# A graph layer on one core: gathering the input itself and normalising the gathered rows on the chip, instead of storing a normalised table first

## The chip, the cores and the metric

The kernel runs on one core of a Trainium2 chip (trn2). The metric is the device time of one execution in microseconds. The kernel before takes 2262.23 us, the median of three runs (2261.8 to 2264.33).

## What is computed

There are 12,500 nodes with rows of 256 numbers (x) and 212,500 edges, sorted by dst, each with a row of 64 numbers. Everything is float32. Cut to what matters:

```python
h = relu(layernorm(x, eps=1e-5))
messages = concat([h[src], edges]) @ W_message          # 320 -> 256
agg = segment_sum(messages, dst)
v = relu(agg) + h
u = layernorm(v) * aggr_scale + aggr_bias
u1 = u + relu(u @ W0 + b0)
u2 = u1 + relu(u1 @ W1 + b1)
w = h + (u2 + u2 @ W2 + b2)
out = x + layernorm(w) * out_scale + out_bias
```

Since the message layer is linear, the kernel first sums the rows of each node (320 numbers: h[src] and the edge row) and multiplies by W_message once for a block of 128 nodes.

## The kernel before

**Names.** A *block* is 128 nodes; there are 98 (NB). A *tile* is 128 edges in the order of dst; there are 1664 (T). Eight tiles (G) are a *group*; there are 208 (NG). A block has some 17 tiles, so its last edge falls into every second group, sometimes the third: that group *closes* the block. The work that follows a closing is a *visit*.

**First stage.** In 14 rounds (NX) of seven rows a partition, POOL loads x (L267), DVE takes mean and variance (`x_moments`: `bn_stats` L572, `bn_aggr` L581) and computes 1/std and the shift with one Newton step in six small operations (`x_scale`, L550 to L564), ACT takes the root (L431) and writes relu((x - mean) / std) in place (L437), and SP stores the rows to a table in HBM, h_table (L240). Between these rounds DVE builds the tables of numbers (`steer`, `whole`) from dst that tell each group in which accumulator each tile goes, whether the group closes a block and which.

**The stream.** When all of h_table is stored (the waits ahead of L274), POOL gathers, for each tile, 128 rows of h_table by src with an indirect DMA (L281) into `ring`, which has room for eight groups (RG); SP loads the edge rows of a group beside them (L248). Both wait for `group_free`, which PE counts up when it has used a group. DVE compares dst with the lane numbers and gets a 128x128 one-hot matrix for each tile (L670); PE multiplies it with the tile (L361) and so adds each edge's row to its node's in PSUM. PE waits for the gathers in pairs of tiles.

**The visits.** Each engine handles a visit in a place of its program that is the same as the group's: in a closing group PE does seven tiles, the visit, and the eighth tile (L372 to L378):

```python
for j in range(G - 1):
    tile(j)
...
with nc.tensor.If(closes > 0):
    pe_visit(pe, visit, ..., close)
tile(G - 1).then_inc(group_free, 1)
```

A visit is a step of a software pipeline over the blocks: it copies the sums of block n, and does each later layer for an earlier block, up to the output of block n - LAG (LAG = 5). PE's part (L301 to L332) transposes z (L305), closes the accumulator (L369), multiplies by W_message (L313), adds the last layer (L319), does two layers (L295) and transposes the sums (L330). ACT's part (`act_visit`) takes the root of the variances (L390), loads h of two blocks and x of one again from HBM (L392 to L395), copies and applies relu (L399 to L417) and stores the output (L406). DVE's part (`dve_visit`) adds, takes both norms with one Newton step, and writes z (L518) and the output (L520). After the last group come a full visit for the last block and LAG short ones.

**What sets the order.** Each engine runs its own program in order, and semaphores join them. DVE makes the one-hots of a group and then, if the group closes a block, does the visit. ACT has nothing but visits. POOL has nothing but gathers.

Of the kernel before, what the change touches and what calls it, by code (L numbers as in the profile page):

```python
# [6 lines left out]
F32 = mybir.dt.float32  # L7
BF16 = mybir.dt.bfloat16
I32 = mybir.dt.int32
# [12 lines left out]
PT = 2  # L22
XS = 4
LAG = 5
# [4 lines left out]
def sizes(n_nodes, n_edges):  # L29
    nb = -(-n_nodes // P)  # L30
    per_load = max(k for k in range(1, 8) if nb % k == 0)
    return nb, per_load, -(-n_edges // (P * GT)) * GT

def build(nc, x, src, dst, edges, w_message, w_mlp, feature_params, row_params, out, NB, XB, T):
# [3 lines left out]
    NX = NB // XB  # L39
    PAIRS = G // PT  # L40

    AT, VSEL, CLOSES, VISIT, TILE, W = G, G + 1, G + 2, G + 3, G + 4, G + 5
    PARAMS = 16 * 5

    h_table = nc.dram_tensor("h_table", (NB * P, D), F32, kind="Internal").ap()
    dump = nc.dram_tensor("dump", (P, D), F32, kind="Internal").ap()
    x_blocks = x.rearrange("(b p) d -> p b d", p=P)
    h_blocks = h_table.rearrange("(b p) d -> p b d", p=P)

    x_rows = x.rearrange("(p b) d -> p b d", p=P)  # L50
    h_rows = h_table.rearrange("(p b) d -> p b d", p=P)
# [3 lines left out]
    with ctx:  # L55
# [11 lines left out]
        close_hot = sb("close_hot", [P, P])  # L67
# [4 lines left out]
        xs = sb("xs", [P, XS, XB, D])  # L72

        flat = ring[:, :, :].rearrange("p j f -> p (j f)")
        dst_i = flat[:, 0:T].bitcast(I32)
        last_i = flat[:, T:2 * T].bitcast(I32)
        last_shifted = flat[:, 2 * T:3 * T].bitcast(I32)
        below = flat[:, 3 * T:4 * T]
        rel = flat[:, 4 * T:5 * T]
        blk_i = sb("blk_i", [1, T + 1], I32)  # L80
# [11 lines left out]
        parity_i = sb("parity_i", [1, NB], I32)  # L92
        parity = sb("parity", [1, NB])
# [4 lines left out]
        visit_sel = sb("visit_sel", [1, NB], I32)  # L98
# [12 lines left out]
        x_stats = sb("x_stats", [P, XB, 6])  # L111
        x_mv = sb("x_mv", [P, 2, XB, 2])
        x_var = sb("x_var", [P, XB])
        x_std = sb("x_std", [P, 2, XB])
        x_y = sb("x_y", [P, XB])
        x_t = sb("x_t", [P, XB])
        x_u = sb("x_u", [P, XB])
        x_rstd = sb("x_rstd", [P, 2, XB])
        x_shift = sb("x_shift", [P, 2, XB])
# [10 lines left out]
        h_in = sb("h_in", [P, D])  # L130
        h_late = sb("h_late", [P, D])
        x_late = sb("x_late", [P, D])
# [6 lines left out]
        w0 = sb("w0", [P, D])  # L139
        w = sb("w", [P, D])  # L140
        scaled = sb("scaled", [P, D])
        o = sb("o", [P, D])
        stats = sb("stats", [P, 2, 6])
        mv = sb("mv", [P, 2, 2])
# [88 lines left out]
        def _(sp):  # L233
# [19 lines left out]
            for s in range(XS):  # L253
                sp.wait_ge(h_stored[s], 16 * len(range(s, NX, XS)))
# [473 lines left out]
```

## Time and profile before

| | |
|---|---|
| median of 3 runs | 2262.23 us |
| the profiled execution | 2263.02 us, of which its span is 2261.2 us |
| mean clock granted to TensorE | 0.937 |
| PE busy, of the span | 74% |
| POOL | 71% |
| DVE | 42% |
| ACT | 16% |
| software DMA queue (the gathers), of 16 engines | 34.7% |

The profile is one execution, recorded on the chip. Times are microseconds from the start of the span unless marked ns. PE is TensorE's matmul, PEld its weight load, DVE is VectorE, ACT ScalarE, POOL GpSimd, SP SyncE; a q behind a name is that engine's queue of instructions that start DMAs.
### The profile page before, as it was taken

What the parts mean: (1) busy time and instruction counts of PE and PEld (TensorE: products, weight loads), DVE (VectorE), ACT (ScalarE), POOL (GpSimd) and SP (SyncE); (2) the same over time, 40 slices, a digit from 0 to 9 for tenths busy, and PEclk for the clock granted to TensorE, in tenths of its full rate; (3) what the DMA queues carried; (4) which work ended last, traced back from release to release, by engine and by line L of the source; (5) the groups of instructions that cost most, each with busy time, mean ns of one, the idle gap of its engine ahead of it and who ended that gap; (6) DMA issues with size and microseconds to landing.
All of it is one profiled execution on the core that took longest, in us unless ns stands there. A gap on an engine that the chain in (4) does not pass through costs nothing.

```text
span 2261.2 us, 35804 instructions
## 1 busy us (share of the span) xinstructions
PE 1672.8 (74%) x6729; PEld 1128.5 (50%) x6730; DVE 957.0 (42%) x3949; ACT 364.2 (16%) x1114; POOL 1594.7 (71%) x1687
## 2 busy tenths in 40 slices
PE   0058778878878777788778778778787887777876
PEld 0035545545555545555555555555554555555544
DVE  8444334434434434443433433443443434434434
ACT  2601111111111111111111111111111111111112
POOL 0067777777777777777777777777777777777770
PEclk9999999999999999999999999998998999999997
DMA  6775555555555555555555555555555555555542
GB/s 234 276 189 158 156 155 155 150 159 155 155 158 154 156 159 150 161 157 149 159 155 155 156 150 161 157 160 149 159 157 151 161 149 158 161 147 161 154 123 61
DMA packets 361302, 357.81 MB, mean 158 GB/s; under 512 B 250208, under 2 KB 303776, under 8 KB 361120
## 3 DMA queue, kind: packets, MB, share of 16 engines
q0 software_dynamic: 81888, 231.06, 34.7%
q1 hardware_dynamic: 218768, 69.94, 12.4%
q10 hardware_dynamic: 60464, 55.28, 7.3%
q14 instruction: 177, 1.45, 0.2%
q8 instruction: 5, 0.08, 0.0%
HBM read 329.65 MB, written 26.48 MB: 157 GB/s over the span
## 4 chain that ended last, share of the span: by engine, by line
POOL 62%; issue 21%; PE 8%; DMA 3%; DVE 1%; POOLq 0%; ACT 0%; DVEq 0%; ACTq 0%
POOL ring L281 62%; PE acc_banks L361 4%; DMA ring<-h_table,src_all 2%; PE agg_bank L313 1%; PE agg_bank L319 1%; PE y_bank L295 1%; PE z_bank L295 1%; PE acc_banks L369 0%; POOLq L277 0%; PE z_bank L305 0%; ACT xs L437 0%; DMA h_table<-xs 0%; PE st_bank L330 0%; POOLq L279 0%; ACT r_bank L411 0%
## 5 line engine op out<-in xcount | busy, mean ns | idle before, releaser
L281 POOL DMA_INDIRECT ring<-h_table,src_all x1664 | 1586.0, 953 | 527.2 <-issue 519.6
L361 PE MATMUL acc_banks<-ring,onehot 128*128 128x320 f32 x3328 | 1112.2, 483 | 518.8 <-issue 310.0
L361 PEld LDWEIGHTS acc_banks<-ring,onehot 128*128 128x128 f32 x3328 | 659.9, 209 | 933.5 <-issue 773.7
L670 DVE TENSOR_SCALAR onehot<-iota,dst_rel 128x128 f32<-128x128 f32 x1664 | 360.6, 303 | 249.2 <-issue 200.7
L480 DVE TENSOR_TENSOR w<-agg_bank,h_late 128x256 f32<-128x256 f32 x103 | 43.7, 424 | 953.8 <-PE agg_bank L319 953.8
L399 ACT ACTIVATE uT<-z_bank,fp 128x128 f32<-128x128 f32 x200 | 80.6, 453 | 1482.0 <-PE z_bank L305 1482.0
L313 PE MATMUL agg_bank<-wm,ST 128*128 128x256 f32 (+1 forms) x594 | 166.4, 401 | 0.0
L313 PEld LDWEIGHTS agg_bank<-wm,ST 128*128 128x128 f32 (+1 forms) x594 | 106.5, 192 | 54.9 <-issue 34.6
L319 PE MATMUL agg_bank<-wl,u 128*128 128x256 f32 x408 | 118.5, 414 | 6.3 <-DVE z L518 6.3
L295 PEld LDWEIGHTS y_bank<-u,wl 128*128 128x128 f32 x808 | 108.8, 196 | 5.6
L295 PE MATMUL y_bank<-u,wl 128*128 128x128 f32 x808 | 109.0, 279 | 0.0
L411 ACT ACTIVATE r_bank<-y_bank,fp 128x128 f32<-128x128 f32 x202 | 60.4, 338 | 298.2 <-PE y_bank L295 298.2
L295 PE MATMUL z_bank<-uT,wl 128*128 128x128 f32 x800 | 106.6, 277 | 0.0
L295 PEld LDWEIGHTS z_bank<-uT,wl 128*128 128x128 f32 x800 | 98.4, 194 | 0.0
L319 PEld LDWEIGHTS agg_bank<-wl,u 128*128 128x128 f32 x408 | 70.8, 193 | 45.8 <-issue 33.1
L369 PE MATMUL acc_banks<-ring,close_hot 128*128 x194 | 74.2, 465 | 0.0
L267 POOL DMA_DIRECT2D xs<-x x14 | 7.6, 549 | 88.9 <-DMA h_table<-xs 88.9
L411 ACT ACTIVATE r_bank<-z_bank,fp 128x128 f32<-128x128 f32 x200 | 59.8, 337 | 30.4 <-PE z_bank L295 30.4
L499 DVE TENSOR_TENSOR u<-u,r_bank 128x256 f32<-128x256 f32 x102 | 42.9, 421 | 20.8 <-ACT r_bank L411 19.9
L572 DVE BATCH_NORM_STATS2 x_stats<-xs 128x6 f32<-128x256 f32 x98 | 37.9, 411 | 30.9 <-DMA xs<-x 30.6
L437 ACT ACTIVATE xs<-xs,x_shift,x_rstd 128x256 f32<-128x256 f32 x98 | 49.4, 585 | 0.0
L520 DVE SCALAR_TENSOR_TENSOR o<-scaled,rstd,xb 128x256 f32<-128x256 f32 x103 | 49.3, 479 | 0.0
(109 smaller groups left out, 919.1 us busy)
## 6 DMA issues: line engine op xcount, KB each, us to landing
ring<-edges SPq DMA_DIRECT2D x208, 256.0 KB, 3.7
ring<-h_table,src_all POOLq DMA_INDIRECT x1664, 2.8
h_late<-h_table ACTq DMA_DIRECT2D x103, 128.0 KB
x_late<-x ACTq DMA_DIRECT2D x103, 128.0 KB
h_in<-h_table ACTq DMA_DIRECT2D x100, 128.0 KB
xs<-x POOLq DMA_DIRECT2D x14, 896.0 KB, 6.5
h_table<-xs SPq DMA_DIRECT2D x14, 896.0 KB, 4.2
out<-o ACTq DMA_DIRECT2D x98, 128.0 KB
```

The costliest lines, as they stand in the source:

```text
L281: nc.gpsimd.indirect_dma_start(out=ring[:, k * G + j, 0:D], out_offset=None, in_=h_table, in_offset=bass.IndirectOffsetOnAxis(ap=src_all[: ...
L295: mm = nc.tensor.matmul(y[layer][:, c * P:(c + 1) * P], wl[:, layer, k, c * P:(c + 1) * P], u[:, k * P:(k + 1) * P], start=(k == 0), stop= ...
L313: mm = nc.tensor.matmul(agg, ST[0:m, c, :], wm[0:m, c, :], start=(c == 0), stop=(c == 2))
L319: mm = nc.tensor.matmul(back, u2[:, k * P:(k + 1) * P], wl[:, 2, k, :], start=(k == 0), stop=(k == 1))
L361: return nc.tensor.matmul(acc_of(at), onehot[:, (k % OG) * G + j, :], ring[:, k * G + j, :], start=False, stop=True, skip_group_check=True)
L369: nc.tensor.matmul(acc_of(sel), close_hot[:, :], rhs, start=False, stop=True, skip_group_check=True).then_inc(block_closed, 1)
L399: op = nc.scalar.activation(uT[:, c * P:(c + 1) * P], zT[:, c * P:(c + 1) * P], ACT.Identity, scale=fp[:, 2, c:c + 1], bias=fp[:, 3, c:c + 1])
L411: op = nc.scalar.activation(r[layer][:, c * P:(c + 1) * P], y[layer][:, c * P:(c + 1) * P], ACT.Relu, bias=fp[:, layer, c:c + 1])
L437: op = nc.scalar.activation(at, at, ACT.Relu, scale=x_rstd[:, n % 2, k:k + 1], bias=x_shift[:, n % 2, k:k + 1])
L480: step(nc.vector.tensor_tensor(w0[:, :], back, h_late[:, :], ALU.add))
L520: nc.vector.scalar_tensor_tensor(o[:, :], scaled[:, :], rstd[:, 1:2], xb[:, :], ALU.mult, ALU.add).then_inc(out_ready, 1)
L670: op = nc.vector.tensor_scalar(onehot[:, (k % OG) * G + j, :], iota[:, :], dst_rel[:, bass.ds(g * G + j, 1)], None, ALU.is_equal)
```

## The change

- There is no first stage and no h_table. POOL gathers rows of x itself, and waits only for src, which SP now loads first.
- Each gathered tile is normalised in `ring`. DVE takes `bn_stats` of its eight tiles (L732) and `bn_aggr` (L739); ACT takes the root (L492) and normalises with relu (`apply`, L463 to L469); the six small operations of `x_scale` are five (`x_norms`: eps is added within the second) and stand between the statistics of the *next* group (`next(norms, None)`). ACT applies them at the head of its next group. PE waits for each half of a normalised group (`applied`), where it waited for pairs of gathers.
- ACT and DVE now walk through all groups. PE handles a visit in the closing group, ACT its middle part (`act_node`) one group later and its norms (`act_norms`) two later, DVE all of its part two groups later (BEHIND = 2).
- In a closing group's visit DVE puts the one-hots of its current group between the steps of the norms (`group_hots`, `next(others, None)`).
- A visit's 1/std is computed on DVE alone, from a first guess of integer arithmetic on the bits (MAGIC) and three Newton steps on three columns; the third is the norm of the block's own rows. ACT writes z, and the h of the block's own rows (`hr`) from x (`xr`), both kept in eight slots (HS) for four visits; only x of one block is loaded in a visit.
- PE adds h and b2 to the last layer by two more matmuls (L319, L320), where DVE did it. LAG is 4. The matmul that closes a block uses a one-hot from four buffers.
- The setup clears `xr`, `hr` and two more tables, and builds those.

The core of the diff:

```diff
-            for n in range(NX):
-                s = n % XS
-                if n >= XS:
-                    pool.wait_ge(h_stored[s], 16 * (n // XS))
-                pool.dma_start(xs[:, s, :, :], x_rows[:, n * XB:(n + 1) * XB, :]).then_inc(x_in[s], 16)
...
+            def gather(g):
+                k = g % RG
+                for j in range(G):
+                    nc.gpsimd.indirect_dma_start(
+                        out=ring[:, k * G + j, 0:D], out_offset=None, in_=x,
+                        in_offset=bass.IndirectOffsetOnAxis(ap=src_all[:, g, j:j + 1], axis=0),
+                    ).then_inc(gathered[2 * k + j // HALF], 16)
+            pool.wait_ge(src_in, 16)
+            for g in range(NG):
+                pool.wait_ge(group_free, g + 1)
+                gather(g)
...
+            def apply(k, count):
+                act.wait_ge(x_norm_ready, count + 2)
+                for j in range(G):
+                    at = ring[:, k * G + j, 0:D]
+                    op = nc.scalar.activation(at, at, ACT.Relu, scale=x_rstd[:, k % 2, j:j + 1], bias=x_shift[:, k % 2, j:j + 1])
+                    if j % HALF == HALF - 1:
+                        op.then_inc(applied, 1)
...
+                        looked = look_back(g)
+                        if not (first and k == 0):
+                            apply((k - 1) % RG, p * NG + g)
+                        act.wait_ge(x_moments_ready, p * NG + g + 2)
+                        nc.scalar.activation(x_std[:, k % 2, :], x_mv[:, k % 2, :, 1], ACT.Sqrt,
+                                             bias=x_eps[:, 0:1]).then_inc(x_std_ready, 1)
+                        visits(*looked)
...
+                        for j in range(G):
+                            if j % HALF == 0:
+                                wait_for(gathered[2 * k + j // HALF], (p * ROUNDS + i + 1) * (16 * HALF))
+                            op = nc.vector.bn_stats(x_stats[:, j, :], ring[:, k * G + j, 0:D])
+                            if j == G - 1:
+                                op.then_inc(x_stats_ready, 1)
+                            next(norms, None)
+                        wait_for(x_norm_ready, count + 1)
+                        wait_for(x_stats_ready, count + 1)
+                        for j in range(G):
+                            op = nc.vector.bn_aggr(x_mv[:, k % 2, j, :], x_stats[:, j, :])
+                        op.then_inc(x_moments_ready, 1)
+                        wait_for(group_free, count + 1 + RG - OG)
+                        with nc.vector.If(closes > 0):
+                            dve_visit(dve, visit, visit * STEPS, slots, group_hots(k, g, opened, tile))
+                            nc.vector.nop()
+                        with nc.vector.Else():
+                            for _ in group_hots(k, g, opened, tile):
+                                pass
+                            nc.vector.nop()
...
+            nc.tensor.matmul(back, ident[:, :], of_slot(hr, late), start=True, stop=False)
+            nc.tensor.matmul(back, ones[0:1, :], b2_row[0:1, :], start=False, stop=False)
+            for k in range(2):
+                mm = nc.tensor.matmul(back, u2[:, k * P:(k + 1) * P], wl[:, 2, k, :], start=False, stop=(k == 1))
```

The new DVE part of a visit, in the order of its code: v (L528), statistics of `back` (L529), then a wait for the last relu (`r_ready`), u2 (L532), statistics of the own rows (L535) and of v (L538), u1 (L541), three `bn_aggr` (L544), xb (L546), the variances (L548), scaled (L549), the first guess (L552), nine Newton operations (L557 to L563), shift (L566), o (L568).

**DVE, from the last Newton step of a visit to the next group.** `rt`, `ru`, `ry`/`rstd` are the small vectors of the norms, `z` goes to the next layer, `o` is the output, `onehot` the one-hots of the group. Before:

```order
L513 SCALAR_TENSOR_TENSOR ru<-rt,ry 128x2 [waits dve_step,tables]
L471 REGISTER_ALU
L515 SCALAR_TENSOR_TENSOR rstd<-ru,ry 128x2 [waits dve_step,tables]
L518 TENSOR_SCALAR z<-v,mv,rstd 128x256 [waits rstd_ready]
L520 SCALAR_TENSOR_TENSOR o<-scaled,rstd,xb 128x256 [waits out_stored]
L680 UNCONDITIONAL_BRANCH
L224 ISA
L224 TENSOR_LOAD steer
L225 ISA
L670 ISA [waits group_free]
L670 TENSOR_SCALAR onehot<-iota,dst_rel 128x128
```

With the change:

```order
L703 TENSOR_SCALAR onehot<-iota,dst_rel 128x128
L519 REGISTER_ALU
L560 SCALAR_TENSOR_TENSOR ru<-rt,ry 128x3 [waits dve_step,tables]
L703 TENSOR_SCALAR onehot<-iota,dst_rel 128x128
L519 REGISTER_ALU
L563 SCALAR_TENSOR_TENSOR ry<-ru,ry 128x3 [waits dve_step,tables]
L519 REGISTER_ALU
L566 SCALAR_TENSOR_TENSOR shift<-mv,ry 128x3 [waits dve_step,tables]
L568 SCALAR_TENSOR_TENSOR o<-scaled,ry,xb 128x256 [waits out_stored,tables]
```

The next group, past the branch, begins so; `x_stats` are the statistics of its gathered tiles and `x_y` is the first of the small vectors for the group before it:

```order
L207 TENSOR_LOAD dve_steer
L208 ISA
L732 BN_STATS x_stats<-ring 128x6 [waits tables,gathered4,x_moments_ready]
L683 RECIPROCAL x_y<-x_std 128x8 [waits x_std_ready,tables]
L732 BN_STATS x_stats<-ring 128x6
```

The one-hots of the group have moved in among the Newton steps, z has gone to ACT, and behind the output stand the next group's statistics with the norms of the group between them.

**PE, inside a visit.** `agg_bank` holds the message layer's result and, in its other half, `back`. Before:

```order
L369 MATMUL acc_banks<-ring,close_hot 128x320
L313 MATMUL agg_bank<-wm,ST 128x256 [waits ST_ready]
L313 MATMUL agg_bank<-wm,ST 128x256 x2
L319 MATMUL agg_bank<-wl,u 128x256 x2
L295 MATMUL y_bank<-u,wl 128x128 x4
L295 MATMUL z_bank<-uT,wl 128x128 [waits u_in]
```

With the change:

```order
L369 MATMUL acc_banks<-ring,close_hot 128x320
L316 MATMUL agg_bank<-wm,ST 128x256 [waits ST_ready]
L316 MATMUL agg_bank<-wm,ST 128x256 x2
L319 ISA
L319 MATMUL agg_bank<-hr,ident 128x256
L320 MATMUL agg_bank<-rows,ones 128x256
L322 MATMUL agg_bank<-wl,u 128x256 x2
L297 MATMUL y_bank<-u,wl 128x128 x4
L297 MATMUL z_bank<-uT,wl 128x128 [waits u_in]
```

Two matmuls now stand ahead of those of the last layer, and so ahead of both layers whose relu DVE waits for.

## Rows read from the trace of the kernel before

**Rows 1.** The page: busy time by engine; chain that ended last, by engine.

```profile
PE 1672.8 (74%) x6729; PEld 1128.5 (50%) x6730; DVE 957.0 (42%) x3949; ACT 364.2 (16%) x1114; POOL 1594.7 (71%) x1687
...
POOL 62%; issue 21%; PE 8%; DMA 3%; DVE 1%; POOLq 0%; ACT 0%; DVEq 0%; ACTq 0%
```

**Rows 2.** Costliest groups: busy us, mean ns | idle before, releaser.

```profile
L281 POOL DMA_INDIRECT ring<-h_table,src_all x1664 | 1586.0, 953 | 527.2 <-issue 519.6
```

**Rows 3.** Timeline of POOL's gathers, first and last: start us, us, line.

```profile
118.88 1.01 POOL L281 DMA_INDIRECT ring<-h_table,src_all  x1 [20.66 <-issue]
...
2210.51 0.95 POOL L281 DMA_INDIRECT ring<-h_table,src_all  x1 [0.30 <-issue]
```

**Rows 4.** DMA issues: count, size, median us from issue to landing.

```profile
ring<-dst SPq DMA_DIRECT2D x2, 832.0 KB, 8.2
...
src_all<-src SPq DMA_DIRECT2D x1, 832.0 KB, 14.3
```

**Rows 5.** Timeline of DVE, setup: first and last table step, keys, one-hots.

```profile
16.67 1.01 DVE L596 TENSOR_SCALAR ring<-ring 128x1664 int32<-128x1664 int32 x1
...
49.01 0.16 DVE L640 CAST whole<-whole_f 1x4 int32<-1x4 f32 x1
...
116.50 1.03 DVE L659 TENSOR_SCALAR dst_rel<-dst_rel 128x1664 f32<-128x1664 f32 x1 [8.89 <-issue]
...
119.10 1.68 DVE L670 TENSOR_SCALAR onehot<-iota,dst_rel 128x128 f32<-128x128 f32 x8 [1.57 <-issue]
```

**Rows 6.** Timeline of DVE and ACT, one round of the first stage.

```profile
19.71 0.43 DVE L572 BATCH_NORM_STATS2 x_stats<-xs 128x6 f32<-128x256 f32 x1
...
21.72 0.14 DVE L564 SCALAR_TENSOR_TENSOR x_shift<-x_mv,x_rstd 128x7 f32<-128x7 f32 x1
...
22.56 0.58 DVE L581 BATCH_NORM_AGGREGATE x_mv<-x_stats 128x2 f32<-128x6 f32 x7
...
23.38 3.54 ACT L437 ACTIVATE xs<-xs,x_shift,x_rstd 128x256 f32<-128x256 f32 x7
```

**Rows 7.** Timeline of PE and ACT, a closing group and its visit.

```profile
1002.51 4.03 PE L361 MATMUL acc_banks<-ring,onehot 128*128 128x320 f32 x14 [1.83 <-issue]
...
1006.11 0.41 PEld L305 LDWEIGHTS z_bank<-ident,z 128*128 128x128 f32 x2
...
1008.77 1.13 PE L319 MATMUL agg_bank<-wl,u 128*128 128x256 f32 x4
...
1011.72 0.60 ACT L411 ACTIVATE r_bank<-z_bank,fp 128x128 f32<-128x128 f32 x2 [0.30 <-PE z_bank L295]
```

**Rows 8.** Timeline of DVE, the same visit and two groups behind it.

```profile
1012.35 0.42 DVE L499 TENSOR_TENSOR u<-u,r_bank 128x256 f32<-128x256 f32 x1 [0.19 <-ACT r_bank L411]
...
1014.26 0.16 DVE L513 SCALAR_TENSOR_TENSOR ru<-rt,ry 128x2 f32<-128x2 f32 x1
...
1014.53 0.16 DVE L515 SCALAR_TENSOR_TENSOR rstd<-ru,ry 128x2 f32<-128x2 f32 x1
...
1015.05 0.48 DVE L520 SCALAR_TENSOR_TENSOR o<-scaled,rstd,xb 128x256 f32<-128x256 f32 x1
...
1016.07 1.70 DVE L670 TENSOR_SCALAR onehot<-iota,dst_rel 128x128 f32<-128x128 f32 x8 [0.54 <-issue]
...
1018.53 1.87 DVE L670 TENSOR_SCALAR onehot<-iota,dst_rel 128x128 f32<-128x128 f32 x8 [0.76 <-issue]
```

**Rows 9.** Timeline of PE, two bursts; a window (granted clock is third last).

```profile
800.98 3.49 PE L361 MATMUL acc_banks<-ring,onehot 128*128 128x320 f32 x12 [2.95 <-issue]
...
1192.66 6.97 PE L361 MATMUL acc_banks<-ring,onehot 128*128 128x320 f32 x14 [2.96 <-issue]
...
1021.90:1028.50 6.60, 6.59 (x14) 4.28 (x15) 0.00 (x0) 0.00 (x0) 5.08 (x6) 0.54 0.38 112
```

**Rows 10.** Timeline, tail: last full visit begins; last output is issued.

```profile
2217.51 0.20 PEld L305 LDWEIGHTS z_bank<-ident,z 128*128 128x128 f32 x2 [0.48 <-issue]
...
2259.09 0.35 ACTq L406 DMA_DIRECT2D out<-o  x1
```

More of the change, by code:

```diff
@@ L206, in build @@
         y_ready = [sem(f"y_ready{k}") for k in range(2)]
-        r_ready = [sem(f"r_ready{k}") for k in range(2)]
+        r_ready = sem("r_ready")
         out_ready = sem("out_ready")
@@ new lines, in _ @@
+            tail = floored(nc.scalar, tail_reg, whole_regs[1])
+            regs = registers(nc.scalar, AW)
+            visit_reg, visit1_reg, new_reg, next_reg, row_reg, load_reg = [
+                nc.scalar.alloc_register(n) for n in ("visit", "visit1", "new", "next", "row", "load")]
+            slots = (new_reg, next_reg, row_reg, load_reg)
+            def apply(k, count):
[5 more added lines that the diff above has]
+                        op.then_inc(applied, 1)
@@ L659, in _ @@
                 nc.vector.tensor_scalar(dst_rel[:, :], dst_rel[:, :], -float(P), None, ALU.add).then_inc(keys_ready, 1)
-                keys = nc.vector.compute_val(p + 1)
-                dve.wait_ge(tables, 1)
-                dve.wait_ge(keys_ready, keys)
-                with nc.vector.Fori(0, ROUNDS) as i:
+                wait_for(keys_ready, p + 1)
+                for i, first in rounds(nc.vector):
                     for k in range(RG):
                         g = i * RG + k
-                        closes, visit, at = numbers(nc.vector, regs, steer_flat, g * W + CLOSES, T)
-                        visit = floored(nc.vector, visit_reg, regs[VISIT - CLOSES])
-                        dve.wait_ge(group_free, p * NG + g + 1 + RG - OG)
+                        count = p * NG + g
+                        norms = x_norms((k - 1) % 2, count) if not (first and k == 0) else iter(())
+                        closes, visit, opened, tile = look_back(g)
+                        wait_for(x_moments_ready, count + 1)
@@ L684, in _ @@
+                for _ in x_norms((NG - 1) % 2, p * NG + NG):
+                    pass
+                for d in range(BEHIND):
+                    closes, visit, opened, tile = look_back(NG + d)
+                    visit_if(closes, visit)
+                dve_visit(dve, nc.s_assert_within(p + tail, 0, NB - 1), (p + tail) * STEPS, slots, iter(()))
+            done = NB * STEPS
             for k in range(1, LAG + 1):
-                dve_visit(dve, NB - 1 + k, last=k)
+                done += dve_visit(dve, NB - 1 + k, done, [None] * 3, iter(()), last=k)
```

558 lines of the change are left out of this document (274 added, 284 removed).

## The prediction

> **What bounds the kernel now.** I read the page first, for the chain that ended last: 62% of it is the gather on POOL (L281) and 21% "issue", the 0.30 us that stand between one gather and the next [rows 1]. The costliest groups then say how many: 1664 gathers of 0.953 us [rows 2]. The timeline of POOL gives their place: the first starts at 118.88, the last ends at 2211.46 [rows 3]. That is 2092.6 us without a hole, 1.2576 us each, 10.06 us for a group of eight. So the time before is 118.9 us until the first gather, 2092.6 us of gathers, and 49 us of tail. Everything else keeps up with POOL. The reader should note what fills the first 118.9 us: the whole of x is normalised and stored to h_table, and no gather may start before that is done.
>
> The profiled execution took 2263.0 us (span 2261.2 and 1.8 around it), 0.8 over the median of 2262.2. I sum against the former and take 0.8 off. A measurement of this kernel can tell about 0.2% (4.5 us) from no change.
>
> **What goes.** The gathers wait only for src. It is now first on SP's queue; third in the queue it landed 14.3 us after issue, the dst load that was first landed after 8.2 [rows 4]. First gather: between 8 and 16 us, I take 10, as it is nearest to the first place. If POOL stayed the bound, the stream would end at 10 + 2093 = 2103, 109 us earlier. That is the whole gain, and it is realised only if the engines behind POOL still keep its pace: 10.06 us for a group, 21.4 us from one closing of a block to the next (97 closings; 96 spacings over 204 groups, hence about 85 of two groups and 11 of three).
>
> **What comes, as busy time.** DVE gets 8 statistics and 8 aggregations a group (7 of each with 6 small operations took 3.43 us [rows 6]), ACT 8 normalisations (7 in 3.54 us [rows 6]), about 4 us each in a group of 10.06. Neither engine fills up: DVE was at 42%, ACT at 16% [rows 1]. By shares the change would win. But shares are not what decides here, the order is.
>
> **The new ring of waits.** Call A the moment at which ACT starts to normalise the tiles of a closing group c. What must happen before the same moment of the next closing group, c+2?
> 1. A to S, where PE begins the visit. Eight normalisations take 3.54 + 0.49 = 4.03, PE wakes 0.06 later, and the three tiles of the second half take 0.51 each (seven tiles from 1002.51 to the visit at 1006.11 [rows 7]). S = A + 5.65.
> 2. S to r, when ACT has written the last relu. Before: 1011.72 + 0.60 - 1006.11 = 6.21 [rows 7]. The change adds two 128x256 matmuls ahead of the layers (L319, L320); two such take 1.13 [rows 7]. r = S + 7.34.
> 3. DVE handles visit c two groups behind, in iteration c+2, and stands at r_ready until r. Behind it: u2, own statistics, statistics of v, u1 (0.34 each, 1.35), three aggregations 0.26, xb 0.32, var 0.07, scaled 0.39, the first guess 0.07, close_hot 0.25; sum 2.71 (pitches from start to start in the old visit; the 0.34 is that of an operation on 256 columns, u for one [rows 8]). Then nine small Newton operations with eight one-hots between: a one-hot has pitch 0.21 (eight in 1.70 [rows 8]), a small operation 0.07, so 2.24 for eight pairs. The last step, and shift, which must wait for it as one small operation waits for the next, 0.26 [rows 8]: shift starts at r + 5.21. o starts at 5.28, ends 0.48 later, and after an o the next group began 0.54 later (15.53 to 16.07 [rows 8]). DVE is in iteration c+3 at r + 6.30.
> 4. Only there, between its statistics of c+3, does DVE compute the norms of group c+2. From the first statistic to the end of x_shift was 21.86 - 19.71 [rows 6], less 0.06 for the dropped x_var: 2.09, and 0.05 to wake ACT.
>
> L = 5.65 + 7.34 + 6.30 + 2.14 = **21.4 us** for two groups, for which POOL needs 20.1. ACT gives no shortcut: after r it has the copies to ST, group c+1 to normalise (4.03), z and the own rows, and is ready at about r + 8, when DVE's norms are at r + 8.4. A third group in a spacing adds DVE's round alone: statistics 3.1, aggregations 0.7, hots 1.9, gap 0.76 (1018.53 after 1017.77 [rows 8]), 6.5 in all, less than POOL's 10.06, so a long spacing gives time back. The mean spacing is L + 0.7, against 21.4 from POOL: already late by 0.7 at every closing, and the ring of eight groups only postpones that.
>
> **PE's clock.** PE now has two idle stretches per closing: from the end of group c to the first half of c+1, and from the end of c+1 to A + 2.1; both come to 2.7 us or so. Before, seven tiles after 2.96 us of idling took 6.97 us, and six after 2.95 us took 3.49; in another slow burst the granted clock was 0.54, near the 1.2 GHz level, from its first tile until the visit 6.6 us later [rows 9]. After 1.83 us of idling seven tiles took 4.03 [rows 7]. So an idle of this length may or may not cost: of the 14 bursts that followed idling of 2.7 to 3.0 us between 300 and 1700 us, seven began at 0.62 of full clock or less, five at 1.00, two between. Half speed at c moves S to A + 2.1 + 6.6 instead of 5.65: 3.1 us more. At c+1 it delays only PE's arrival, about 1.2. I take 4 in 10 for each stretch, a little under that count, as these are at its short end: 0.4 x 1.2 + 0.6 x 0.4 x 3.1 = 1.2 us.
> Page "TensorE: Matmul & The Clock Gate" of the Trainium skill (section "What's actually happening") says that TensorE falls back to 1.2 GHz when it has idled and gets 2.4 GHz only by being busy; by that rule every closing group would run slow. Here the trace agrees for one of the two rows of rows 9 and not for the other.
>
> **Registers.** ACT and DVE load more numbers a group, and each of DVE's steps has a register row. The trace prices none apart: not below 0, and not above the difference of the two gaps of rows 8, 0.22, in each of two iterations. I take 0.2 in all. L = 21.4 + 1.2 + 0.2 = **22.8 us**.
>
> **Head and tail.** The tables were ready at 49.2, with 32.4 us of setup from 16.67 [rows 5], of which 10 were three rounds of x statistics. Now memsets and the loads hold DVE until about 11; 22.4 of setup, 4.9 for clearing hr and the new tables, 2 for dst: 40. From dst_rel to the first one-hot 2.6 [rows 5]. Three DVE rounds and 2.1 later, A of the first closing group (2) is at 63. Bounds 55 and 72. The tail before was 41.9 from the last full visit (2217.51 to 2259.44 [rows 10]) with five short ones behind. Now four, but each has two more matmuls at the low clock (2.2), three Newton rounds (1.1 more) and a trip to ACT for z (0.5): I take 58, bounds 48 and 65.
>
> **The sum.** 63 + 85 x 22.8 + 11 x 29.3 = 2323 for A of the last closing group (205), 22.8 more to the last group, 6 to its visit, 58: 2410 + 1.8 - 0.8 = **2411 us**, 6.6% slower than before. Each tenth of a microsecond in L is worth 9.7 us. The gain of 109 us at the start is real and eaten by a queue of gathers that stands before a full ring.
>
> **The rivals.**
> - *POOL stays the bound* (the other side: faster). Then 10 + 2093 + 3 to land + 9 to the visit + 58 + 1 = **2174 us**. For it: both busy shares leave room, and my ring misses POOL's pace by only 4%. It needs L of 20.6 or less; between 20.6 and 21.2 the result is in between, still faster; 21.25 is break-even. Against it: every term of the 21.4 is a measured pitch, none is a guess, and the clock can only add. Chance 0.20, and 0.04 for landing on break-even.
> - *The ring at full clock.* L = 21.4: 2411 - 97 x 1.4 = **2275 us**. For it: the burst of six tiles at full speed. Chance 0.13.
> - *The ring with PE slow at every closing group.* L = 24.5 + 0.2: 2411 + 97 x 1.9 = **2595 us**. For it: 2.96 us of idling was enough. Chance 0.13. It is the case that the clock page of the Trainium skill describes.
> - *Gathers made slower by the added statistics*, or a start that doesn't come early because src is late: each moves the first rival only, by 1664 x 0.06 = 100 us at most (a gather took 1.01 instead of 0.95 at its first [rows 3]). It is inside the chances above.
>
> The forecast (a ring of 22 to 23.7 us) has 0.50. Range: 2195 to 2530; below lies the better half of the POOL case, above most of the slow-clock case. Faster 0.20, same 0.04, slower 0.76.
>
> **What would show it.** Right: the chain that ended last goes through DVE, PE and ACT, POOL's share of it falls below a quarter, POOL waits for PE (group_free) over 200 us in all, and visits of PE stand 22 to 23.5 us apart for two groups. PE's mean granted clock falls below 0.93. DVE's first relevant wait in a visit is for the relu. Wrong: gathers still stand 1.2576 apart to the end (then step 3 or 4 was too long), or the spacing is right and the head above 72 or the tail above 65.

## Result: 14% slower, and the profile after

The changed kernel takes **2575.99 us** (median, 2570.37 to 2579.07), the kernel before took 2263.28 beside it: ratio 1.1375 (95% interval 1.1359 to 1.1391), slower by 313 us. The forecast was 2411, range 2195 to 2530: the direction is right, the time lies outside the range, and the change costs twice what was forecast.

The page: busy time by engine, the chain that ended last, the gathers (answers to [rows 1, 2]).

```profile
PE 1863.2 (72%) x7137; PEld 1260.9 (49%) x7138; DVE 1727.1 (67%) x8735; ACT 1264.4 (49%) x2968; POOL 1586.7 (62%) x1672
...
PE 47%; issue 16%; DVE 13%; ACT 10%; ACTq 8%; DVEq 4%; DMA 0%; SPq 0%
...
L268 POOL DMA_INDIRECT ring<-x,src_all x1664 | 1585.8, 953 | 853.1 <-issue 477.7
```

POOL, 62% of the chain before, is gone from it. No engine is busy more than 72%, a gather still takes 0.953 us, and the chain runs through PE, DVE and ACT in turn: a ring of waits, not a full engine. The waits (engine, what waited, for what: us, times, longest):

```profile
PE acc_banks L362 <- ACT ring L467: 648.1, 195, 11.4
...
DVE v L528 <- PE agg_bank L322: 390.2, 98, 8.7
POOL ring L268 <- PE acc_banks L362: 369.9, 95, 10.0
...
ACT ring L467 <- DVE x_shift L695: 289.7, 105, 6.3
...
DVE u L532 <- ACT r_bank L403: 152.5, 101, 3.0
```

The start and the end, from the timeline (answers to [rows 3, 10]): first and last gather; ACT starts to normalise group 2, the first that closes; PE begins the last full visit; the last output.

```profile
7.09 1.87 POOL L268 DMA_INDIRECT ring<-x,src_all  x1 [5.51 <-DMA src_all<-src]
...
62.33 4.04 ACT L467 ACTIVATE ring<-ring,x_shift,x_rstd 128x256 f32<-128x256 f32 x8 [2.02 <-DVE x_shift L695]
...
2439.46 0.95 POOL L268 DMA_INDIRECT ring<-x,src_all  x1 [0.30 <-issue]
...
2515.67 0.41 PEld L308 LDWEIGHTS z_bank<-ident,z 128*128 128x128 f32 x2
...
2574.56 0.48 DVE L568 SCALAR_TENSOR_TENSOR o<-scaled,ry,xb 128x256 f32<-128x256 f32 x1
```

Gathers start 112 us earlier than before, at 7.09. A of the first closing group is at 62.33 (63 was forecast), the tail takes 2577.2 - 2515.7 = 61.5 (58). Both ends are right within 4 us. The miss lies between: the 97 closings are (2499.27 - 68.32)/96 = 25.3 us apart on the mean, where 23.5 was forecast.

One *lap* of the ring, from a visit of PE to its next, in the timeline (answers to [rows 7, 8]). PE begins visit c at 1080.91 and visit c+2 at 1105.93:

```profile
1080.91 0.41 PEld L308 LDWEIGHTS z_bank<-ident,z 128*128 128x128 f32 x2
...
1087.72 0.60 ACT L403 ACTIVATE r_bank<-z_bank,fp 128x128 f32<-128x128 f32 x2 [0.29 <-PE z_bank L297]
...
1088.42 0.42 DVE L532 TENSOR_TENSOR u<-u,r_bank 128x256 f32<-128x256 f32 x1 [1.51 <-ACT r_bank L403]
...
1094.20 0.48 DVE L568 SCALAR_TENSOR_TENSOR o<-scaled,ry,xb 128x256 f32<-128x256 f32 x1
...
1095.40 0.43 DVE L732 BATCH_NORM_STATS2 x_stats<-ring 128x6 f32<-128x256 f32 x1 [0.72 <-issue]
...
1097.62 0.15 DVE L695 SCALAR_TENSOR_TENSOR x_shift<-x_mv,x_rstd 128x8 f32<-128x8 f32 x1
...
1098.26 4.04 ACT L467 ACTIVATE ring<-ring,x_shift,x_rstd 128x256 f32<-128x256 f32 x8 [2.88 <-DVE x_shift L695]
...
1100.64 4.64 PE L362 MATMUL acc_banks<-ring,onehot 128*128 128x320 f32 x10 [4.04 <-ACT ring L467]
...
1105.93 0.41 PEld L308 LDWEIGHTS z_bank<-ident,z 128*128 128x128 f32 x2
```

This is the ring of the prediction, step by step, in 25.02 us. The next lap, at full clock, took 23.02 (to 1128.95), where 21.4 was forecast for full clock. Three things are to be seen.

First, after x_shift ends (1097.77) ACT starts only 0.49 later. The chain that ended last, cut out for this stretch (start us, us, what), says why:

```profile
1094.09 0.17 DVE shift L566
1094.63 0.11 ACTq L424
1094.81 0.11 ACT hr L419
1095.02 0.37 ACTq L426
1095.69 0.36 ACTq L433
1096.13 0.38 issue
1096.60 1.27 ACTq L207
1098.03 0.18 ACTq L208
1098.26 1.37 ACT ring L467 x3
```

There is a second way round, as long as that through DVE: from DVE's shift through ACT's z and hr, two DMA issues, and the load of five numbers from the steering table (L207), 1.27 us. The wait is booked on x_shift, but ACT's own queue came last. In 63 of the first 94 laps (of 96), ACT started over 0.2 us after x_shift.

Second, the burst at 1100.64, after 4.04 us of idling, began at the lower clock; the one of the next lap, after 2.07, did not. The windows of the two (the length, then PE busy; the granted clock is third last: 1.00 is 2.4 GHz throughout; the 0.63 is 0.52, near the 1.2 GHz level, up to 1104.0 and 0.93 from there to 1105.28, so the full clock was back before the visit):

```profile
1100.63:1105.28 4.65, 4.64 (x11) 3.15 (x12) 4.15 (x19) 1.86 (x5) 3.43 (x4) 0.63 0.38 115
1123.50:1129.00 5.50, 3.65 (x14) 2.63 (x15) 4.71 (x28) 3.69 (x9) 4.00 (x5) 1.00 0.66 164
```

Third, once in eight groups DVE and ACT jump back to the top of their loops. The first statistic and the first normalisation of such a round:

```profile
409.04 0.43 DVE L732 BATCH_NORM_STATS2 x_stats<-ring 128x6 f32<-128x256 f32 x1 [3.71 <-issue]
...
412.74 4.04 ACT L467 ACTIVATE ring<-ring,x_shift,x_rstd 128x256 f32<-128x256 f32 x8 [6.71 <-issue]
```

DVE's gap before the statistics has a median of 3.70 us at the first group of a round, and of 0.14 to 0.51 at the other seven. There are 24 such jumps: round 0 stands ahead of the loop. ACT's gap before the first normalising behind a jump is of two kinds. In eleven of the 24 it is 2.8 to 3.1 us and nothing that the profile shows is waited for, where such gaps have a median of 0.9 or less elsewhere. In the other thirteen it is 5.3 to 6.7 (hence the 5.31 in the median), and eleven of these are booked on DVE's x_shift, so that DVE's own jump is in them.

The kernel before had this gap too, where it cost nothing. Its one-hots at the first group of a round, and at the next group:

```profile
1081.15 1.78 DVE L670 TENSOR_SCALAR onehot<-iota,dst_rel 128x128 f32<-128x128 f32 x8 [4.71 <-issue]
1083.58 1.92 DVE L670 TENSOR_SCALAR onehot<-iota,dst_rel 128x128 f32<-128x128 f32 x8 [0.65 <-issue]
```

All 25 jumps of DVE there show 3.8 to 5.2 us, and the medians of the other seven groups are 0.6 to 0.9.

### The profile page after: what moved, and what is told of

Same layout as the page of the kernel before. It is cut to its first block, busy times and chain, and to the rows that moved or that the text cites. A ratio compares the mean times of both kernels' runs of the same rounds, so it can differ in the third digit from the quotient of the medians.

```text
span 2577.2 us, 50916 instructions
## 1 busy us (share of the span) xinstructions
PE 1863.2 (72%) x7137; PEld 1260.9 (49%) x7138; DVE 1727.1 (67%) x8735; ACT 1264.4 (49%) x2968; POOL 1586.7 (62%) x1672
## 4 chain that ended last, share of the span: by engine, by line
PE 47%; issue 16%; DVE 13%; ACT 10%; ACTq 8%; DVEq 4%; DMA 0%; SPq 0%
PE acc_banks L362 22%; ACT ring L467 7%; PE agg_bank L316 6%; PE agg_bank L322 4%; ACTq L207 4%; PE y_bank L297 4%; PE z_bank L297 4%; PE agg_bank L319 3%; PE agg_bank L320 3%; ACT r_bank L403 2%; PE acc_banks L369 2%; DVE rt L557 1%; DVE ru L560 1%; ACTq L433 1%; DVE onehot L703 1%
## 5 line engine op out<-in xcount | busy, mean ns | idle before, releaser
L268 POOL DMA_INDIRECT ring<-x,src_all x1664 | 1585.8, 953 | 853.1 <-issue 477.7
L362 PE MATMUL acc_banks<-ring,onehot 128*128 128x320 f32 x3328 | 1182.7, 515 | 648.1 <-ACT ring L467 648.1
L362 PEld LDWEIGHTS acc_banks<-ring,onehot 128*128 128x128 f32 x3328 | 735.6, 228 | 1059.9 <-issue 903.4
L467 ACT ACTIVATE ring<-ring,x_shift,x_rstd 128x256 f32<-128x256 f32 x1664 | 840.2, 587 | 415.5 <-DVE x_shift L695 289.7
L732 DVE BATCH_NORM_STATS2 x_stats<-ring 128x6 f32<-128x256 f32 x1664 | 638.9, 412 | 169.2 <-issue 159.5
L703 DVE TENSOR_SCALAR onehot<-iota,dst_rel 128x128 f32<-128x128 f32 x1664 | 414.6, 305 | 0.0
L528 DVE SCALAR_TENSOR_TENSOR v<-agg_bank,hr 128x256 f32<-128x256 f32 x99 | 42.1, 425 | 390.9 <-PE agg_bank L322 390.2
L739 DVE BATCH_NORM_AGGREGATE x_mv<-x_stats 128x2 f32<-128x6 f32 x1664 | 133.6, 153 | 27.5
L532 DVE TENSOR_TENSOR u<-u,r_bank 128x256 f32<-128x256 f32 x101 | 42.5, 421 | 152.5 <-ACT r_bank L403 152.5
L699 DVE TENSOR_SCALAR close_hot<-iota,block_start,dst_f 128x128 f32<-128x128 f32 x208 | 75.9, 365 | 50.4 <-issue 49.9
L416 ACT ACTIVATE z<-v,shift,ry 128x256 f32<-128x256 f32 x99 | 59.3, 599 | 55.7 <-DVE shift L566 55.7
L319 PE MATMUL agg_bank<-hr,ident 128*128 (+1 forms) x204 | 73.2, 441 | 8.5 <-DVE shift L566 8.5
```

Source lines behind the costliest of these rows:

```text
L268: nc.gpsimd.indirect_dma_start(out=ring[:, k * G + j, 0:D], out_offset=None, in_=x, in_offset=bass.IndirectOffsetOnAxis(ap=src_all[:, g, j ...
L319: nc.tensor.matmul(back, ident[:, :], of_slot(hr, late), start=True, stop=False)
L362: return nc.tensor.matmul(acc_of(at), onehot[:, (k % OG) * G + j, :], ring[:, k * G + j, :], start=False, stop=True, skip_group_check=True)
L467: op = nc.scalar.activation(at, at, ACT.Relu, scale=x_rstd[:, k % 2, j:j + 1], bias=x_shift[:, k % 2, j:j + 1])
L703: op = nc.vector.tensor_scalar(onehot[:, (k % OG) * G + j, :], iota[:, :], dst_rel[:, bass.ds(g * G + j, 1)], None, ALU.is_equal)
L732: op = nc.vector.bn_stats(x_stats[:, j, :], ring[:, k * G + j, 0:D])
```

## Experiments

Twelve kernels. "Ring": the time is the length of the ring times its laps. "Load": it is what the engines have to do, at the clock they get, and no one wait sets it.

**1. Visits of DVE and ACT three groups behind instead of two**, so that DVE never meets the relu.

```
-BEHIND = 2
+BEHIND = 3
-  (dve_steer, 2, D_CLOSES, D_VISIT), (act_steer, 2, A_CLOSES, A_VISIT)
+  (dve_steer, BEHIND, D_CLOSES, D_VISIT), (act_steer, BEHIND, A_CLOSES, A_VISIT)
```

> ACT's norms and DVE's part of a visit come three groups behind the closing group instead of two, so that DVE computes the norms of group c+2 before it waits for visit c. Theory 'ring' (the time is 97 turns of one chain of waits: normalise c, PE's visit, last relu, DVE's visit, norms of c+2): the chain is cut, what is left is ACT's own round of about 20 us for two groups and POOL's 20.1, so the spacing of PE's visits falls from 24.7 to about 20.5 us and the time from 2576 to 2180 to 2280 us. Theory 'load' (DVE, ACT and PE with their gaps cannot keep POOL's pace in any order): the same work in another order stays above 2540 us.

Measured: 2895.07 us (ratio 1.2764, 1.2722 to 1.2807). Slower by 319; both theories missed it. Its waits, and one lap of its timeline:

```profile
DVE x_y L684 <- ACT x_std L492: 785.9, 101, 12.1
```
```profile
1021.00 0.60 ACT L403 ACTIVATE r_bank<-z_bank,fp 128x128 f32<-128x128 f32 x2 [0.29 <-PE z_bank L297]
...
1022.93 4.04 ACT L467 ACTIVATE ring<-ring,x_shift,x_rstd 128x256 f32<-128x256 f32 x8 [0.88 <-issue]
...
1026.87 0.28 ACT L492 ACTIVATE x_std<-x_mv,x_eps 128x8 f32<-128x8 f32 x1
...
1027.26 0.20 DVE L684 RECIPROCAL x_y<-x_std 128x8 f32<-128x8 f32 x1 [5.94 <-ACT x_std L492]
...
1038.20 0.60 ACT L416 ACTIVATE z<-v,shift,ry 128x256 f32<-128x256 f32 x1 [4.85 <-DVE shift L567]
...
1039.34 0.20 PEld L308 LDWEIGHTS z_bank<-ident,z 128*128 128x128 f32 x2 [4.32 <-ACT hr L419]
```

The wait for the relu is gone and a longer ring has closed in its place, through ACT's in-order queue: last relu, then a whole group normalised (4.04), then the root that DVE needs for its next norms, then DVE's statistics and visit, then ACT's z, then PE. That is a theory; run 5 tests it.

**2. The loops over rounds of PE, ACT and DVE written out.**

```
-  for i, first in rounds(nc.vector):
+  for i, first in [(i, i == 0) for i in range(ROUNDS)]:
```

> The loop over rounds of eight groups is written out for PE, ACT and DVE, all else is as in the changed kernel. In the trace of the changed kernel DVE stands 3.7 us before the first group of a round and 0.1 to 0.7 before the others, ACT 5.3 instead of 2. Theory 'ring' with the jump back as one of its terms: 25 jumps of some 3.5 us lie on the chain, about -90 us (2490). If the jumps fall into slack they cost under 20 us. Theory 'load': they are part of the load as well, -75 to -90 us, so this run separates jump from no jump, not ring from load.

Measured: 2511.42 us (ratio 1.1086, 1.1048 to 1.1123): 65 off, where about 90 was expected. The jumps cost 0.7 us a lap on the mean.

**3. The two added matmuls left out** (L319, L320).

> The two matmuls that add h and b2 ahead of the last layer are left out (the output lacks h and b2 there). They take 1.25 us of PE in a visit. Theory 'ring': they stand between A and the last relu in each of 97 turns, -120 us (2455). Theory 'load': PE is busy 72% and would only have more idle, under 20 us.

Measured: 2423.38 us (ratio 1.0707, 1.0674 to 1.0740): 153 off, more than the ring by itself gives. The table at the end of this section says where most of the rest came from.

**4. Filler for PE's clock**: eight small matmuls with zeros at the head of each group.

```
+  for _ in range(8):
+      nc.tensor.matmul(acc_of(0), zero_w[:, :], zero_row[:, :], start=False, stop=True, skip_group_check=True)
```

> Eight bf16 matmuls of zeros (320 columns, about 1.1 us together) are added to the accumulators at the head of each group, in the idle stretch before PE waits for the normalised tiles. If the half clock after idling is the cause of the mean 6.9 us from A to PE's visit (6.0 at best): it falls to 6.0 to 6.1, mean clock from 0.90 to above 0.97, -85 us (2490). If the filler is too short or the clock is not on the chain: no change, or slower by what it delays, up to +30 us.

Measured: 2591.94 us (ratio 1.1442, 1.1409 to 1.1476): 16 more. The mean granted clock rose from 0.898 to 0.913, but not where it counts: 43 of 94 closing bursts (those that end in a visit) came at the lower clock (41 in the changed kernel), as the filler stands ahead of the wait for ACT and the idling comes behind it. In eight more, at full clock, PE came late and took 7.7 to 8.2 us from A to the visit, against 5.98 where it is on time. So this run shows what the filler costs; what the clock costs at the closing bursts it leaves untested, as it did not change it there.

**5 to 8, on one chip.** Run 5 is run 1 with ACT's root ahead of its normalising:

```
-  if not (first and k == 0):
-      apply((k - 1) % RG, p * NG + g)
   act.wait_ge(x_moments_ready, p * NG + g + 2)
   nc.scalar.activation(x_std[:, k % 2, :], x_mv[:, k % 2, :, 1], ACT.Sqrt,
                        bias=x_eps[:, 0:1]).then_inc(x_std_ready, 1)
+  if not (first and k == 0):
+      apply((k - 1) % RG, p * NG + g)
```

> The version with visits three steps behind, with one more edit: ScalarE takes the root of group g before it applies the norms of group g-1, not after. Theory 'ScalarE's queue is in the chain': the visits three steps behind were slower because VectorE's next statistics need a root that stands behind ScalarE's 4.04 us of applying, which itself stands behind the relus of the node work (786 us of waits for that root). With the root first the chain from one closing to the next is 7.4 (visit to last relu) + 0.3 (root) + 5.8 (statistics, norms, aggregates) + 0.3 + 6.0 (apply to the next visit) = about 19.8, against about 29 measured there and 24.7 in the changed kernel: 2895 falls to 2100 to 2300, with GpSimd's issue chain (about 2174) as a floor; VectorE's wait for the root under 250 us. Rival 'load': the order of waits is not what counts, the clock and the amount of work are: 2860 to 2900.

Measured: 2359.99 us (ratio 1.0426, 1.0409 to 1.0444): 535 below run 1, 60 over the expected band. Moving one instruction did it, as the theory of run 1 says; the wait for x_std is 249.9 us instead of 785.9. Nothing was taken from the load.

Run 6 is the changed kernel with its two matmuls behind the two layers:

```
-        back = agg_bank[:, D:2 * D]
+        back = row_bank[:, D:2 * D]
...
-            nc.tensor.matmul(back, ident[:, :], of_slot(hr, late), start=True, stop=False)
-            nc.tensor.matmul(back, ones[0:1, :], b2_row[0:1, :], start=False, stop=False)
...
                 pe_layer(0, uT)
+            nc.tensor.matmul(back, ident[:, :], of_slot(hr, late), start=False, stop=False)
+            nc.tensor.matmul(back, ones[0:1, :], b2_row[0:1, :], start=False, stop=True).then_inc(back_ready, 1)
...
-            stats_done = step(nc.vector.bn_stats(stats[:, 1, :], back))
...
                 nc.vector.tensor_tensor(u1[:, :], uT[:, :], r[0], ALU.add)
+            after(back_ready, n + 1)
+            stats_done = step(nc.vector.bn_stats(stats[:, 1, :], back))
```

> The changed kernel with its two added matmuls (the kept rows and the bias of the last layer) moved behind the node's two layers and into a bank of their own, nothing left out; VectorE takes the statistics of that sum last. Theory 'ring': the last relu comes 1.25 us earlier, VectorE gets back 0.8 us of it (it meets the moved matmuls after 1.7 us of its own first operations): 97 visits x 0.8 = 80 us off, 2480 to 2520. Rival 'load': the same matmuls are done, so 2560 to 2585.

Measured: 2450.55 us (ratio 1.0827, 1.0807 to 1.0846): 125 off, where 80 was expected, with every matmul still done. Where two matmuls stand in the queue is worth most of what they cost.

Run 7 is run 5 with the edit of run 2:

> As e5_root_first, and the loops over rounds of TensorE, ScalarE and VectorE written out. 'ScalarE's queue in the chain', and loop jumps cost: another 30 to 65 us below e5_root_first, unless GpSimd's issue (floor about 2174) has become the bound, and then under 30. 'Load': 2800 to 2850.

Measured: 2296.38 us (ratio 1.0142, 1.0122 to 1.0161), 64 below run 5. One lap, ACT and DVE, of its timeline:

```profile
1005.07 0.36 PEld L308 LDWEIGHTS z_bank<-ident,z 128*128 128x128 f32 x2
...
1011.95 0.60 ACT L403 ACTIVATE r_bank<-z_bank,fp 128x128 f32<-128x128 f32 x2 [0.30 <-PE z_bank L297]
...
1012.73 0.27 ACT L410 ACTIVATE ST<-st_bank 64x128 f32<-64x128 f32 x1
...
1013.77 0.30 ACT L490 ACTIVATE x_std<-x_mv,x_eps 128x8 f32<-128x8 f32 x1 [0.78 <-issue]
...
1014.17 0.20 DVE L684 RECIPROCAL x_y<-x_std 128x8 f32<-128x8 f32 x1 [2.67 <-ACT x_std L490]
...
1018.37 0.42 DVE L529 SCALAR_TENSOR_TENSOR v<-agg_bank,hr 128x256 f32<-128x256 f32 x1 [0.66 <-issue]
...
1024.78 0.60 ACT L416 ACTIVATE z<-v,shift,ry 128x256 f32<-128x256 f32 x1 [2.65 <-DVE shift L567]
...
1025.92 0.20 PEld L308 LDWEIGHTS z_bank<-ident,z 128*128 128x128 f32 x2 [0.32 <-ACT hr L419]
```

20.85 us, where 19.8 was worked out: the same ring as in run 1, shorter by the group that ACT no longer normalises in it.

Run 8 is run 7 with the edit of run 6:

> Visits three behind, root first, loops written out, and the two matmuls late. 'Ring': at GpSimd's floor, 2165 to 2230, whatever the two matmuls are worth; GpSimd's waits for a free group under 60 us. 'Load': above 2700.

Measured: 2306.10 us (ratio 1.0181, 1.0163 to 1.0200). A miss: 76 us over its band, and 10 us above run 7. The lap above shows why nothing was gained: in this ring the root stands behind the two ST copies, and these wait for PE's transposes of the sums. The two matmuls, in their late place, still stand ahead of those transposes. A cut is worth something only on the ring that closes last, and run 6 cuts another one. Where the 10 us come from is not shown.

**9 to 12, on one chip.** Run 9 is run 7 with the root of the next group inside the node work, behind the copy to S_cur, where ACT idles 4 us for PE:

```
   nc.scalar.activation(S_cur[:, :], acc_of(sel), ACT.Copy).then_inc(block_saved, 1)
+  if between is not None:
+      between()
...
+  def root(p, g):
+      act.wait_ge(x_moments_ready, p * NG + g + 2)
+      nc.scalar.activation(x_std[:, g % 2, :], x_mv[:, g % 2, :, 1], ACT.Sqrt,
+                           bias=x_eps[:, 0:1]).then_inc(x_std_ready, 1)
```

> As e7_root_first_unrolled, but ScalarE takes the root of the next group inside the node work, after it has copied the closed sums out, where it waits 4 us for TensorE, and no longer behind the relus and the two ST copies. Theory 'ScalarE's queue in the chain': VectorE's wait for the root (323 us) goes under 80 us and the chain closes through ScalarE's own order instead: relus and copies (7.9 after the visit's start), two groups applied (8.6), the visit's norms and hr (1.2) and TensorE's start (0.3) = about 18 to 19.5 instead of 20.85 measured there. 96 x 1.5 to 2.5 = 140 to 240 off 2296, of which GpSimd's issue floor leaves only what is above 2174: 2165 to 2215, below the kernel before. Rival 'load': 2285 to 2300, unchanged.

Measured: 2203.95 us (ratio **0.9745**, 0.9730 to 0.9760): faster than the kernel before.

Run 10 is run 9 with the edit of run 6:

> e9_root_in_node with the two matmuls late. If e9 is at GpSimd's issue floor, the same within 10 us; if TensorE or ScalarE still bound it, up to 60 us less.

Measured: 2194.42 us (ratio **0.9705**, 0.9691 to 0.9718), the fastest of all. Its chain, and POOL in its waits and timeline:

```profile
POOL 41%; PE 34%; issue 17%; ACTq 3%; ACT 2%; DVE 2%; DMA 0%; DVEq 0%
```
```profile
POOL ring L269 <- PE acc_banks L363: 3.4, 11, 0.3
```
```profile
7.28 1.69 POOL L269 DMA_INDIRECT ring<-x,src_all  x1 [5.70 <-DMA src_all<-src]
...
2099.14 0.94 POOL L269 DMA_INDIRECT ring<-x,src_all  x1 [0.30 <-issue]
```

Gathers run without a hole from 7.28 to 2100.08, 2092.8 us, as in the kernel before, whose stream began at 118.88 [rows 3]. This is the prediction's first rival, at last, with its stream as it had it, but POOL is not the only bound: the chain is POOL's up to 1197 us and goes through PE behind that, and the time from the last gather to the end is 94 us where the rival had 70. Run 9's gathers end at the same time (2099.7), so the 10 us between the two runs lie behind the last gather, and the expectation of run 10 holds.

The expectation of run 9 had one thing wrong: short spacings stayed at 20.8 us, and DVE still waited 174 us for the root. The gain is in the eleven spacings of three groups among the 94 (33.1 to 25.6 us, 82 of the 92 us). The traces show both. In a long spacing the root of the second group comes 8.6 us behind PE's visit in run 7 and 1.7 in run 9, and what follows from it to PE's next visit takes about as long as before (24.5 and 23.9). In the short ones the root comes as much earlier, but another way round has closed there: in run 9 the chain of such a lap (1010 to 1033 us) goes from the last relu through ACT's copies to the first half of the next group, and then through fifteen tiles that PE does without a pause (30 instructions, 9.93 us at 1021.84). So PE's own work is in the ring now.

Run 11 is the changed kernel with the edits of runs 2 and 6:

> The changed kernel (visits two behind) with its loops written out and the two matmuls late: both cuts lie on the same chain at different places, so they add: 2576 - 65 - 125 = 2386, between 2360 and 2410. If either gain was a matter of load or of the clock, they would not add: 2420 to 2450.

Measured: 2347.86 us (ratio 1.0385, 1.0368 to 1.0402), 228 below the changed kernel and 38 more than the two gains apart. By the table below, some 21 us of the 38 stand in A to S, which falls by 0.86 where the two apart give 0.64. The rest is DVE's gap at the jump: run 6 had made it longer (start of o to statistics 5.7 us at the 13 visits ahead of a jump, 4.3 in the changed kernel), and here it is gone.

Run 12 drops one of the three Newton steps:

```
-            for k in range(3):
+            for k in range(2):
                 of, to = ry[(k + 1) % 2], ry[k % 2]
```

> The changed kernel with two Newton steps instead of three for the node's 1/std (three dependent operations of VectorE less in each visit, 0.23 apart; the result of the root is less precise). Theory 'ring': VectorE's part from relu to output is 0.65 to 0.75 shorter, 97 x 0.7 = 68 off: 2495 to 2525. Rival 'load': VectorE is busy 67% and does 0.16 x 3 x 101 = 48 us less, which nothing waits for: 2565 to 2580. The one-hots between the steps are done anyway, so what they covered may stay: then up to 30 less only.

Measured: 2480.00 us (ratio 1.0969, 1.0951 to 1.0986): 96 off for three small operations, more than expected. So the steps of DVE are on the ring too.

The terms of the prediction, from each trace: means over the first 94 laps, S the start of PE's visit, A ACT's start on the closing group. The sum can differ from the spacing a little, since it takes in long laps too.

```
                        forecast  after  run 2  run 3  run 6  run 12  run 11
A to S                    6.85     6.91   6.83   6.67   6.35   6.48    6.05
S to last relu            7.34     7.41   7.42   6.16   6.16   7.42    6.16
relu to start of o        5.28     5.92   5.76   5.91   6.37   5.01    6.24
start of o to statistics  1.02     1.67   1.09   1.67   1.86   1.99    1.09
statistics to A           2.14     2.63   2.78   2.59   2.57   2.56    2.64
spacing, two groups       22.8    24.71  24.02  23.12  23.46  23.61   22.17
A to S within 6.15, laps    -      43     53     54     71     66      92
```

Each cut appears in its own row (runs 3 and 6: 1.25 in row 2; run 2: 0.58 in row 4; run 12: 0.91 in row 3, of which 0.32 comes back behind it), run 6 gives 0.45 back in row 3, where DVE now takes the statistics of the late sum, and every cut lets row 1 fall as well. Of the 94 closing bursts 41 were at the lower clock in the changed kernel, 34 in run 3, 16 in run 6 and 2 in run 11. That is most of the part of run 3 that the ring at a fixed clock does not give: a cut of 1.25 us took 1.59 off the spacing, 0.24 of it in row 1. The prediction's worth of a tenth of a microsecond in L, 9.7 us, held: 1.59 x 97 = 154 for 153 measured.

## Why the prediction was wrong, step by step

- **What bounds it, what goes, the head and the tail: right.** 62.33 for 63, 61.5 for 58; the spacings are 84 of two groups and 12 of three for 85 and 11 (which make 203 groups only; the last closing group is 206, not 205). First gather 7.1 instead of 10: src landed 6.1 us after issue.
- **The ring, steps 1 to 4 in their order: right.** Shown by runs 3, 6 and 12, which shorten PE's and DVE's parts, by run 2, and by the timeline.
- **What failed is the size of L, above all steps 3 and 4**, each too short because it was summed from pitches of other code:
  - step 3, relu to start of o: 5.92 for 5.28. The pitches were taken from the old visit, which has other operations between other waits; 0.64 us are missing over some 25 operations. Which of them are slower I did not single out.
  - the gap behind o: 1.67 from the start of o for 1.02. Of the 0.65, 0.58 is the loop: run 2 has 1.09. The 13 visits ahead of a jump have 4.33, the others 1.24. The prediction had no term for the loop at all, though the trace of the kernel before had 3.8 to 5.2 us at each jump.
  - step 4: 2.63 for 2.14. "ACT gives no shortcut, ready at r + 8" failed here. Behind the relus ACT has z, hr, two DMA issues and a load of five numbers from the table, and z waits for the very shift of DVE that the prediction had in step 3. It was ready at r + 9.9 in the lap above, and set A in two laps of three. x_shift ended 2.19 after the first statistic (2.09 was forecast), and A came 0.44 behind it instead of 0.05: 0.39 of the 0.49 us is ACT's own queue.
  - together 1.78 us; step 2 (7.41 for 7.34) and A to S (6.91 for 6.85) are right within 0.07, and the 0.2 for registers is inside the three terms. The 96 spacings of both kinds took 25.32 us on the mean for 23.54: 171 us. The first visit came 1.5 us early, from the last closing to the last full visit it was 5.5 less and the tail 3.5 more: 167 in all, which is the profiled run (2579.07) less the sum before its last step (2411.9).
- **PE's clock: A to S was right by luck.** 41 of 94 closing bursts began slow (4 in 10 was taken), but each cost 1.9 us (7.90 for 5.98), not 3.1. The prediction had half the clock up to the visit. In 31 of the 41 the full clock was back before the visit and the burst took 5.0 to 5.3 us; in ten it came later and the burst took 6.0 to 6.7. In all 41 PE stood waiting for ACT. On the other side A to S at full clock and on time is 5.98, not 5.65, and in eleven laps PE came late at full clock (6.8 on the mean), which the prediction did not have. So 5.65 + 1.2 stands against 5.98 + 0.93. Idling before the bursts at full clock was 2.6 us at most and 1.8 on the mean (of the 42 with PE on time), before the slow ones 4.5 on the mean, and over 3 in all but two. The page "TensorE: Matmul & The Clock Gate" of the Trainium skill ("What's actually happening") says that the throttled clock is the default and that activity releases it, which the prediction took to mean slow at every closing group; here the trace agrees for the long stretches of idling only.
- **The rival at 2595** (slow at every closing) has nearly the right time for the wrong reason: fewer than half of the bursts were slow, and 41 of them at 1.9 us are some 80 us of the 313.
- **The rival at 2174 (POOL stays the bound) was drawn too near.** It needed L of 20.6, and looked near because L at full clock was summed to 21.4, 4% over POOL's pace. It was 23.0 in the lap behind the one shown and 23.8 on the mean of the 46 short laps whose closing burst was at full clock. That every term is a measured pitch did not make the sum complete.
- **What would show it:** POOL's share of the chain, its 370 us of waits and the clock of 0.898 came as said; the spacing (24.7) did not. DVE's first wait in a visit is for PE's sum (390 us) and the relu comes second (152 us); only the relu's counts, as nothing is behind the first but work that fits in before it.

## What to carry to other kernels

When a change turns stages that followed one another into one loop over several engines, write down every way round the loop, the one through each engine's own queue included, and not only the one that looks longest: here two ways were nearly equally long, and cutting one (run 1) let a third close that was longer than both. Sum the laps from rows of the new code's kind, add the gaps of jumps and of register loads (look for them in the trace of the kernel before, also where they cost nothing there), and take the sum as a lower end: of five terms three were short by 0.5 to 0.65 us and none was long. And before a piece of work is taken out of such a ring, look whether it can stand elsewhere in the queue: moving a root and two matmuls, with the visits one group later and the loops written out, turned 14% slower into 3% faster, with nothing left out.

## What the runs showed of the chip

- A jump back over a round of eight groups holds DVE for 3.7 us before its next instruction (median; 4.7 in the kernel before), where it has 0.14 to 0.51 ahead of the other groups. ACT has 2.9 behind a jump where it waits for nothing else, and 0.9 or less elsewhere. Written out, DVE's issue gaps before the statistics fell from 159 to 60 us in all. The page "Runtime: NRT & Kernel Launch" of the Trainium skill ("Instruction fetch mechanics") says that a taken branch to a page that isn't held must fetch it first. The trace agrees: packets of the DMA queues that the profile calls `instruction` start in each of the 24 gaps of DVE behind a jump, in 31 of the 182 before the statistics of other groups, and in 3 of the same 25 places when the code is written out. Which engine such a packet is for, the trace doesn't say.
- A load of five numbers into registers took ACT 1.27 us on the chain.
- Two matmuls of 256 columns added to the visit, one of 128 rows and one of a single row, took 1.25 us together, by row 2 of the table.
- Filler that raised the mean granted clock (0.898 to 0.913) made the kernel slower, while run 3, with a lower mean (0.882), was faster: the mean says little, the clock of the burst on the ring says it.
